# One-hots of a histogram on another engine, in a two-layer graph network kernel

## The reference, cut to what matters

```
h = relu(layernorm(x));  x = x + attention0(h, edges)   # 8 heads of 8, bias edge_attr_8,
                                                        # softmax over the edges of each dst
h = relu(layernorm(x));  x = x + transformer(h, edges)  # two layers, 4 heads of 32,
                                                        # segment sums over src, layer norm
```

## Time and profile before

| | us |
|---|---|
| timed runs, median of 3 (2748.7 to 2753.51) | 2752.41 |
| profiled execution, span of its records | 3469.1 |

### The profile page before, as it was taken

One profiled execution on the slowest core, in us unless ns is written; L12 is line 12 of the kernel. 1 busy time (PEld: TensorE's weight loads), 2 busy tenths in 40 slices (PEclk: granted clock), 3 DMA queues, 4 the chain that ended last, 5 costly groups with the idle time before them and its releaser, 6 DMA issues.

```text
span 3469.1 us, 40007 instructions
## 1 busy us (share of the span) xinstructions
PE 2000.1 (58%) x10636; PEld 1656.2 (48%) x10636; DVE 1794.3 (52%) x6283; ACT 1137.1 (33%) x3025; POOL 1708.5 (49%) x1751
## 2 busy tenths in 40 slices
PE   5655555565335565553496366666666366666766
PEld 4433333343233333332484366566665366666765
DVE  9645454455546776556993243343347233334336
ACT  8322222232104544442113133333334133323333
POOL 0455544545566665663001656556561665655650
PEclk7555555555557777777697566666667566666666
DMA  2000000000222222222002333333342333333331
GB/s 69 3 4 3 4 3 3 4 3 3 76 72 62 63 65 61 64 63 27 1 2 79 96 98 101 101 98 102 96 100 71 100 100 96 102 103 95 103 98 25
DMA packets 114125, 209.58 MB, mean 60 GB/s; under 512 B 46138, under 2 KB 57212, under 8 KB 113532
## 3 DMA queue, kind: packets, MB, share of 16 engines
q0 software_dynamic: 69632, 146.42, 15.6%
q1 hardware_dynamic: 44284, 60.61, 5.7%
HBM read 193.30 MB, written 13.60 MB: 60 GB/s over the span
## 4 chain that ended last, share of the span: by engine, by line
another core or an unknown queue 23%; PE 17%; DVE 12%; issue 8%; ACT 3%; POOL 0%; DMA 0%; DVEq 0%; ACTq 0%; POOLq 0%
PE PS L1391 6%; PE PS L1164 4%; DVE work L1317 3%; PE PS L1401 3%; ACT kv L748 2%; DVE red L1322 2%; DVE work L1309 1%; DVE work L1334 1%; PE PS L760 1%; PE PS L1403 1%; DVE work L739 1%; PE PS L1516 1%; PE PS L1249 1%; DVE work L1038 0%
## 5 line engine op out<-in xcount | busy, mean ns | idle before, releaser
L1297 POOL DMA_INDIRECT arena<-kv_d,S x528 | 516.3, 978 | 338.6 <-DVE work L1334 189.9
L666 POOL DMA_INDIRECT sorted_d<-S,rows x416 | 415.4, 999 | 484.6 <-DVE rows L536 357.8
L1391 PE MATMUL PS<-arena,work 128*128 x1760 | 383.6, 386 | 448.4 <-DVE work L1317 417.8
L1297 POOL DMA_INDIRECT kv<-kv_d,S x352 | 343.2, 975 | 500.1 <-DMA kv_d<-arena 266.9
L1391 PEld LDWEIGHTS PS<-arena,work 128*128 128x128 f32 x1760 | 333.3, 282 | 479.8 <-issue 479.8
L923 POOL DMA_INDIRECT kv<-kv_d,S x440 | 424.6, 965 | 274.5 <-issue 132.5
L1401 PE MATMUL PS<-work,R 128*128 128x128 f32 x1760 | 525.9, 392 | 37.8 <-issue 34.9
L1358 ACT ACTIVATE R<-iota,gate 128x128 f32<-128x128 f32 x880 | 279.8, 388 | 747.8 <-remote 663.1
L1403 PEld LDWEIGHTS PS<-wts,R 128*128 128x128 f32 x1760 | 376.9, 262 | 73.2 <-issue 72.5
L1401 PEld LDWEIGHTS PS<-work,R 128*128 128x128 f32 x1760 | 381.6, 266 | 33.7 <-issue 32.6
L760 PE MATMUL PS<-kv,work 128*128 128x440 f16 x832 | 230.5, 436 | 255.2 <-DVE work L739 179.5
(11 more groups left out here) (272 smaller groups left out, 3361.7 us busy)
## 6 DMA issues: line engine op xcount, KB each, us to landing
work<-segT_d SPq DMA_DIRECT2D x165, 256.0 KB
kv<-kv_d,S POOLq DMA_INDIRECT x792
arena<-kv_d,S POOLq DMA_INDIRECT x528
sorted_d<-S,rows POOLq DMA_INDIRECT x416
kv_d<-arena SPq DMA_DIRECT2D x12, 512.0 KB, 2.9
sorted_d<-S SPq DMA_DIRECT2D x1, 2200.0 KB, 8.5
S<-sorted_d SPq DMA_DIRECT2D x1, 2040.0 KB, 8.8
work<-in_edge_attr_dram SPq DMA_DIRECT2D x1, 1660.0 KB
```

The lines of the kernel that those rows point to most:

```text
L666: gp.indirect_dma_start(out=sorted_d, out_offset=bass.IndirectOffsetOnAxis(ap=rows0[0:n, c:c + 1], axis=0), in_=S0[0:n, c, :], in_offset=N ...
L1297: gp.indirect_dma_start(out=ring[s][:, j, :], out_offset=None, in_=kv1_d[l], in_offset=bass.IndirectOffsetOnAxis(ap=S1[:, t, 1:2], axis=0) ...
L1391: done = nc.tensor.matmul(banks[7][:, j * DM:(j + 1) * DM], RT[:, g % 2, j * P:(j + 1) * P], table[:, ds(blocks[g % 3][j] * (3 * DM), DM)] ...
```

## The change

The high one-hots of the histogram are made on GpSimd, column by column, against a float32 copy `khi_f` of the high digits. ScalarE makes the low ones of every fourth group, VectorE those of the other three. The payload copies move to GpSimd, behind group 52 of its one-hots. The span and block tables (`ge0`, L583, L585, `tables0_vector`) move into the rank loop: `ge0` ahead of group 10 (`LATE`), the matmuls in group 11, the tables ahead of group 12. The one-hots of the rank loop are unchanged.

```diff
+LATE = 10
+        khi_f = back1[:, :]
-        SPAN = banks[6][0:1, 0:HI]
+        SPAN = banks[7][0:1, 480:480 + HI]
         def keys_vector(dve):
...
+            nc.vector.tensor_copy(khi_f, digit_i)
-        def payload_vector(dve):
-            dve.wait_ge(s_key, 1)
-            dve.wait_ge(s_fill, 16)
-            nc.vector.tensor_scalar(S0[:, 0:EC, 0:1], dst1.unsqueeze(2), 1.0, None, ALU.add)
-            nc.vector.tensor_copy(S0[:, 0:EC, 1:2].bitcast(i32), src1.unsqueeze(2)).then_inc(s_pay, 1)
+        def payload_gpsimd(gp):
+            gp.wait_ge(s_ends, 64)
+            gp.wait_ge(s_attr, 32)
+            gp.wait_ge(s_fill, 16)
+            nc.gpsimd.tensor_scalar(S0[:, 0:EC, 0:1], dst1.unsqueeze(2), 1.0, None, ALU.add)
+            nc.gpsimd.tensor_copy(S0[:, 0:EC, 1:2].bitcast(i32), src1.unsqueeze(2)).then_inc(s_pay, 1)
+            nc.gpsimd.tensor_copy(S0[:, 0:EC - 1, 2:W0P], attr[:, 0:EC - 1, :])
+            nc.gpsimd.tensor_copy(S0[0:TAIL, EC - 1, 2:W0P], attr[0:TAIL, EC - 1, :]).then_inc(s_paya, 1)
 
         def sort_vector(dve):
             for g in range(NEG):
-                since(dve, s_ohu, g - AHEAD + 1)
-                done = highs(high16[:, g % AHEAD, :, :], g)
-                if g % 3 < 2:
-                    done = lows(low16[:, g % AHEAD, :, :], g)
-                done.then_inc(s_oh, 1)
-
-            payload_vector(dve)
+                if g % 4 < 3:
+                    since(dve, s_ohu, g - AHEAD + 1)
+                    lows(low16[:, g % AHEAD, :, :], g).then_inc(s_oh, 1)
+
...
-            vstep(nc.vector.tensor_copy(look[:, 1:2], STARTS))
-            nc.vector.tensor_tensor(ends0, look[:, 1:2], tiles_f, ALU.add).then_inc(s_look0, 1)
-            dve.wait_ge(s_look0, 1)
-            nc.vector.tensor_scalar(ge0, iota_t[0:HI, :], ends0, None, ALU.is_ge).then_inc(s_ge0, 1)
-
-            tables0_vector(dve)
+            nc.vector.tensor_copy(look[:, 1:2], STARTS).then_inc(s_look0, 1)
+
             for g in range(NEG):
+                if g == LATE:
+                    dve.wait_ge(s_look0, 1)
+                    vstep(nc.vector.tensor_tensor(ends0, look[:, 1:2], tiles_f, ALU.add))
+                    nc.vector.tensor_scalar(ge0, iota_t[0:HI, :], ends0, None, ALU.is_ge).then_inc(s_ge0, 1)
+                if g == LATE + 2:
+                    tables0_vector(dve)
...
             pe.wait_ge(s_look0, 1)
-            nc.tensor.matmul(SPAN, look[:, 1:2], ident[0:HI, 0:HI], start=True, stop=True)
-            pe.wait_ge(s_ge0, 1)
-            nc.tensor.matmul(BLOCKS0, ones[0:HI, :], ge0, start=True, stop=True).then_inc(s_blk0, 1)
-            pe.wait_ge(s_span, 1)
             transposes(0, 0)
             for g in range(NEG):
                 b = g % 2
+                if g == LATE + 1:
+                    nc.tensor.matmul(SPAN, look[:, 1:2], ident[0:HI, 0:HI], start=True, stop=True)
+                    pe.wait_ge(s_ge0, 1)
+                    nc.tensor.matmul(BLOCKS0, ones[0:HI, :], ge0, start=True, stop=True).then_inc(s_blk0, 1)
...
+        def highs_gpsimd(gp):
+            gp.wait_ge(s_key, 1)
+            for g in range(NEG):
+                since(gp, s_ohu, g - AHEAD + 1)
+                for j in range(EG):
+                    c = g * EG + j
+                    done = nc.gpsimd.tensor_scalar(high16[:, g % AHEAD, j, :], iota16[:, 0:HI], khi_f[:, c:c + 1],
+                                                   None, ALU.is_equal)
+                done.then_inc(s_high, 1)
+                if g == NEG // 2:
+                    payload_gpsimd(gp)
```

More of the change, by code:

```diff
@@ L49 @@
 assert (2 + AHEAD) * EG * P // 2 <= (NP - 1) * T
+assert NEG % 4 == 0 and AHEAD == 4
 assert NB % CB == 1 and N % P and ENDS[-1] == NEG and NPAD - N < P
@@ L269, in build @@
         s_low = sem("s_low")
+        s_high = sem("s_high")
         s_scan = sem("s_scan")
@@ L560, in sort_tensor @@
             for g in range(NEG):
-                pe.wait_ge(s_oh, g + 1)
-                k = g // 3
-                if g % 3 == 2:
+                pe.wait_ge(s_high, g + 1)
+                k = g // 4
+                if g % 4 < 3:
+                    pe.wait_ge(s_oh, 3 * k + g % 4 + 1)
+                else:
                     pe.wait_ge(s_low, k + 1)
@@ L566, in sort_tensor @@
                     done = count(high16[:, g % AHEAD, j, :],
-                                 near16[:, k % 2, j, :] if g % 3 == 2 else low16[:, g % AHEAD, j, :])
+                                 near16[:, k % 2, j, :] if g % 4 == 3 else low16[:, g % AHEAD, j, :])
                 done.then_inc(s_ohu, 1)
@@ L575, in transposes @@
             def transposes(g, b):
-                pe.wait_ge(s_oh, NEG + g + 1)
+                pe.wait_ge(s_oh, 3 * NEG // 4 + g + 1)
                 since(pe, s_ats, g)
@@ L607, in sort_tensor @@
                         transposes(g + 1, 1 - b)
[L609 to L614, removed]
         def lows_scalar(act):
             act.wait_ge(s_key, 1)
-            for k in range(NEG // 3):
-                since(act, s_ohu, 3 * (k - 1))
+            for k in range(NEG // 4):
+                since(act, s_ohu, 4 * (k - 1))
                 for j in range(EG):
-                    c = (3 * k + 2) * EG + j
+                    c = (4 * k + 3) * EG + j
                     done = nc.scalar.activation(near16[:, k % 2, j, :], iota16[:, :], ACT.Abs, scale=-1.0,
@@ L677, in group_vector @@
         def group_vector(dve):
+            dve.wait_ge(s_pay, 1)
             vstep(nc.vector.tensor_scalar(word_i, src1, 7, None, ALU.logical_shift_right))
@@ L901, in project0_scalar @@
         def project0_scalar(act):
+            act.wait_ge(s_paya, 1)
             for b in range(NB):
@@ L1561, in _ @@
             constants_gpsimd(gp)
+            highs_gpsimd(gp)
             scatters_gpsimd(gp)
@@ L1595, in _ @@
             lows_scalar(act)
-            payload_scalar(act)
             sort_scalar(act)
```

## The result

| | before | after |
|---|---|---|
| median, us | 2749.27 (5 runs) | 2866.09 (5 runs, 2860.73 to 2868.32) |
| ratio, 95% interval | | 1.0413 (1.0401 to 1.0426) |

The change costs 117 us. The forecast was +36 us, the range ended at 2830 us. The direction was right, the size was not.

The account below looks back on a forecast made before the run. VectorE and ScalarE bound the histogram, VectorE's path the sort. Histogram 96.7 + 6.4 - 66.6 = +36.5 us, the rest -0.3: +36 us on 2752.41, 2789 us; range 2736 to 2830 us.

Parts of the forecast that it names:

- What bounds: Whole sort: VectorE and ScalarE fill the histogram; VectorE's path ends the sort, GpSimd some 3 us behind.
- The lock: Histogram: VectorE's lows and GpSimd's compares exclude each other, so a period costs the sum, 3.72 us; 53%.
- The compare: Histogram: each of 416 GpSimd compares of 32 elements costs 0.12 us, or 0.19 as the dearer value.
- The payload: Mid-histogram, after group 52: copies on GpSimd cost 4.5 to 8.5 us, taken 6.4.
- khi_f: Before the keys are released: one more cast, +0.4 us.
- The tables: Block tables moved into the rank loop: 7.6 us gained, 6.9 given back, net -0.7 us.
- GpSimd's queue offers no cover: Rank loop, groups 12 to 15: batch needed at 170.9, ready at 169.8 us, so GpSimd cannot hide the tables.
- (a): Histogram rival: no lock, cheap compares, two full engines relieved; 2742 us; 27%.
- (b): Histogram rival: no lock, compares at 0.19 us, GpSimd alone bounds; +18.5 us, 2771 us; 12%.
- (c): Histogram rival: no lock, compares of 0.13 to 0.16 us, gain and loss cancel within 5.5 us of 2752; 8%.
- (d): Rival on the sort's end: GpSimd's scatters end it, tables alone matter; shifts each case by up to -7 us.

Follow-up runs that it names:

- the repeated profile: The kernel before, profiled once more without an edit, for a profile without the long pauses: one run of 2745.22 us, span 2743.4 us.

## Why the prediction was wrong

**What bounds.** The histogram as two full engines was right. The claim that VectorE's path ends the sort by 3 us was wrong: in the repeated profile the DMAs of keys and values are issued by 646 us and the last scatter starts at 657.80. The working put GpSimd's end at 635.5 from 16 x 1.26 us a batch, the spacing of two scatters; on average a scatter takes 993 ns and has 0.33 us before it, 1.32 us, because some are longer and three have pauses of over 3 us before them. This error moved only the small term of the tables.

**The lock.** Right, and shown: it cost 0.54 us a low (0.60 taken), went away when one operand left SBUF, and made a low of 5.08 us beside the copies. Its rows had been of another pair of instructions, as it says itself; for this pair the runs here are the first to show it.

**The compare.** This is the step that failed: "so 0.12 us at 32 elements, which I take", with 0.19 as the dearer value. It measured 0.33. 16 x 0.33 + 3 x 0.54 = 6.90 us a period instead of 3.72, so the sum had 26 x (6.90 - 3.72) = 83 us too little (87 for the compares, 5 too much for the lock), against the miss of 117 - 36 = 81. The interpolation of the iotas was good for an iota (0.103 us); the error was to price an operation by another one of the same engine. The prediction gave an upper bound of 1.26 us, then chose by nearness of width, not of kind, and closed its range at 0.21 us a compare. The estimate from the Trainium skill ("GPSIMD Engine Reference", Performance pitfalls for Q7 kernels), 0.2 us, lay nearer but also short. That section prices a small read command of a kernel on this engine's cores, and the prediction laid it on the iota as the price of reading. The runs don't bear that out: a copy, which reads the tile, takes 0.05 us more than an iota (0.152 against 0.103), and a constant scalar saves nothing.

**The payload.** The prediction has 6.4 us; the copies held GpSimd for 5.8, and without them the histogram is 4.5 us shorter.

**khi_f.** VectorE starts its first one-hots at 9.62 instead of 9.35 us: 0.3 for 0.4.

**The tables.** The transposes were to come 7.6 us earlier and came 7.67 earlier (10.30 to 2.63 us). Of this 6.9 us were to be given back. On VectorE all of it was (its loop ends at 611.20 and 611.19 us), on GpSimd, which ends the sort, 5.7, so that 1.3 us are left where the prediction had 0.7. The term was right within the noise; the 3.8 us at the load are mostly other differences of the two traces. The statement that GpSimd's queue offers no cover was right for group 12 and wrong for the loop: at group 80 it covers everything.

**The rivals.** (a), two engines relieved, needed a compare under 0.145 us and no lock; both fail. (b) had the right bound, GpSimd, with too cheap a compare. (c) needed a compare of 0.13 to 0.16 us. (d) was right that GpSimd's scatters end the sort, but with the tables at group 12 this gains only 1.3 us of its 7. Without lock and payload the kernel still loses 74 us.

## What to carry to other kernels

Price an instruction that no row shows by a row of the same operation on the same engine, or leave the range as wide as the bounds: rows of another operation gave 0.12 us for 0.33. What an idle engine costs is the number of instructions times its own price for each, and 416 of them made it the bound at once; a quarter of that, placed where a slower engine's period has room, was harmless. A stretch of one engine's work that must go somewhere goes where another engine's queue is longest: the same tables cost 5.7 us of GpSimd's time at groups 10 to 12 and nothing at groups 80 to 82.

## What the runs showed of the hardware

A compare on GpSimd costs about 0.27 us plus 1.9 to 2.6 ns an element (0.287 us at 8 elements, 0.579 at 128), a copy of 32 elements 0.15 us, an iota 0.10. A VectorE compare of 512 elements a partition with both inputs in SBUF delays GpSimd's compares by 0.54 us (0.46 where these are 64 wide), and GpSimd's copies keep it out until they end (5.08 us for 0.69); with one input in PSUM both run on (groups of 1.33 us, lows of 0.69). TensorE's granted clock is 0.50 in the rank loop of the kernel before (the lower of its two levels, 1.2 GHz) and 1.00 in the changed one (2.4 GHz). Ahead of the loop, in the histogram, TensorE was 70% busy in the kernel before (46.63 of 66.60 us, clock 0.82) and 34% in the changed one (63.12 of 183.49 us, clock 1.00). The rank loop is no faster for the higher clock:

```profile
250.00:550.00 300.00, 249.81 (x1080) 164.97 (x1080) 236.50 (x1366) 130.11 (x420) 224.12 (x229) 0.50 0.04 5
```

is the kernel before in its repeated profile, and the changed kernel is

```profile
250.00:550.00 300.00, 245.21 (x1059) 161.53 (x1059) 236.20 (x1348) 126.77 (x410) 220.72 (x225) 1.00 0.04 5
```

Both take 4.39 us for a group without rows (310.00 to 314.39 and 307.15 to 311.53, from one one-hot to the next). The changed kernel has 21 matmuls fewer in its stretch because the tables, at 262 to 267 us, lie in it.
